# Delta net in a perceiver: the block inverse stops two quarters early, and a correction product takes the place of a transposition

## What is computed

```
q, k, v = silu(conv4(x @ W_qkv))            # q, k normalised to length 1
g = -exp(A_log) * softplus(a + dt_bias);  beta = sigmoid(b)
for t in range(S):                          # state: 128 x 128 per value head
    state = state * exp(g[t])
    delta = (v[t] - k[t] @ state) * beta[t]
    state = state + outer(k[t], delta)
    out[t] = q[t] @ state
y = rmsnorm(out) * norm_w * silu(x @ W_z);   x = x + y @ W_out
```

## Time and profile before

| | before |
|---|---|
| median of 3 runs | 1622.51 us (1621.43 to 1623.59) |
| profiled execution, time | 1629.97 us |
| profiled execution, span | 1628.0 us |
| PE busy | 1514.2 us, 93% |
| DVE busy | 1102.7 us, 68% |
| ACT busy | 607.5 us, 37% |
| POOL busy | 597.1 us, 37% |
| mean granted PE clock | 0.974 |

### The profile page before, as it was taken

How to read it: one execution, slowest core, us unless ns; L and a number is a source line. 1 busy time by engine, 2 the same in 40 slices (tenths; PEclk the granted TensorE clock), 3 DMA queues, 4 the chain that set the end, 5 groups by cost and what they waited for, 6 DMA issues and landing times. The chain is left out here.

```text
span 1628.0 us, 34641 instructions
## 1 busy us (share of the span) xinstructions
PE 1514.2 (93%) x14528; PEld 1075.3 (66%) x14528; DVE 1102.7 (68%) x1726; ACT 607.5 (37%) x1028; POOL 597.1 (37%) x935
## 2 busy tenths in 40 slices
PE   6799599999987889999999999999999978999999
PEld 3344278877964557777777677777777765555556
DVE  4767576687567677887788877788787834543433
ACT  3333353345343444344444445444444431111110
POOL 1201143254234457555564546645566421000000
PEclk9999899999998899999999999999999998999999
DMA  8533200110000222121211222112121114100000
GB/s 227 159 105 93 65 1 2 27 27 1 1 1 21 56 50 49 35 49 40 57 46 36 48 44 57 45 36 49 43 57 44 24 28 159 56 1 0 13 1 13
DMA packets 142347, 75.81 MB, mean 47 GB/s; under 512 B 111920, under 2 KB 123440, under 8 KB 140400
## 3 DMA queue, kind: packets, MB, share of 16 engines
q1 hardware_dynamic: 142192, 73.60, 17.6%
HBM read 55.73 MB, written 17.83 MB: 45 GB/s over the span
## 5 line engine op out<-in xcount | busy, mean ns | idle before, releaser
L1894 DVE SCALAR_TENSOR_TENSOR W<-PS,wc,W 128x504 f32<-128x504 f32 x375 | 274.8, 733 | 88.2 <-ACT W L1574 79.3
L1574 ACT ACTIVATE W<-PS,wc 128x512 f32<-128x512 f32 x125 | 85.8, 686 | 173.0 <-PE PS L1269 115.0
L2234 PE MATMUL PS<-HT,wgu 128*128 128x512 f32 x320 | 143.5, 593 | 0.0
L1269 PE MATMUL PS<-HT,wv 128*128 128x512 f32 x252 | 125.1, 620 | 3.4 <-DVE W L1894 3.4
L1441 PE MATMUL PS<-wo,ogT 128*128 128x256 f32 x512 | 119.1, 392 | 7.6 <-DVE dl L1958 5.1
L1292 PE MATMUL PS<-wz,HT 128*128 128x256 f32 x512 | 123.4, 389 | 0.6 <-DMA wz<-in_gdn_w 0.6
L1269 PE MATMUL PS<-HT,wkq 128*128 128x512 f32 x248 | 121.1, 613 | 0.8 <-DVE W L1894 0.8
L2368 DVE SCALAR_TENSOR_TENSOR act<-th,PS 128x512 f32<-128x512 f32 x48 | 33.0, 687 | 128.2 <-ACT th L2294 128.2
L1441 PEld LDWEIGHTS PS<-wo,ogT 128*128 128x128 f32 x512 | 98.6, 195 | 23.9 <-DVE dl L1958 5.3
L1794 POOL TENSOR_TENSOR rr<-nm,con 128x8 f32<-128x8 f32 x16 | 26.5, 1658 | 233.0 <-DVE nm L1923 233.0
L1578 ACT ACTIVATE W<-W 128x512 f32<-128x512 f32 x125 | 78.2, 626 | 89.7 <-DVE W L1894 89.7
(11 more groups left out here) (275 smaller groups left out, 3113.0 us busy)
## 6 DMA issues: line engine op xcount, KB each, us to landing
a_rows<-AT SPq DMA_DIRECT2D x16, 512.0 KB, 2.6
wk<-in_l0x_k SPq DMA_DIRECT2D x16, 384.0 KB, 3.8
wgu<-in_moe_gu SPq DMA_DIRECT2D x5, 1024.0 KB, 15.8
queries_scratch<-tts SPq DMA_DIRECT2D x32, 128.0 KB, 2.7
wkq<-in_gdn_w SPq DMA_DIRECT2D x16, 256.0 KB, 2.8
wv<-in_gdn_w SPq DMA_DIRECT2D x16, 256.0 KB, 2.8
wz<-in_gdn_w SPq DMA_DIRECT2D x16, 256.0 KB, 3.3
wo<-in_gdn_w SPq DMA_DIRECT2D x16, 256.0 KB, 2.9
```

Source lines behind the costliest of these rows:

```text
L1269: mm = pe.matmul(PS[:, qbank(h, q), :], w[:, o:o + DK], HT[:, k, f * 512:(f + 1) * 512], start=(k == 0), stop=(k == DC - 1))
L1574: a.activation(acc[:, flows(h, q), :], PS[:, qbank(h, q), :], ACT.Copy, scale=wc[:, h % 2, 4 * c + 3:4 * c + 4]).then_inc(s["tap"], 1)
L1894: v.scalar_tensor_tensor(a0, p0, wc[:, h % 2, 4 * c + 2 - k:4 * c + 3 - k], a0, ALU.mult, ALU.add).then_inc(s["conv"], 1)
L2234: mm = pe.matmul(PS[:, 2 * (i % 2) + w, :], pack[:, k, w, :], HT[:, k, f * N:(f + 1) * N], start=(k == 0), stop=(k == DC - 1))
```

## The change

The second transposition product and the second growing round go. Instead:

- all products of 64x64 matrices loop over n, b, hv, with the output of hv = 1 in the opposite half (`place`), so that four successive ones lie in four quarters; `cross` and `grow` write banks 6 and 7, one for each value head;
- the upper blocks of T alone are taken into `mix` (as if T were final but for the lower left 32x32 quarter), `lower_cross` makes the product that `cross(j, 5)` made, ACT keeps it (`keep_lower`, mask now with the sign -1) and keeps the rear 32 columns of the mixed product as `Zs` (`keep_Z`), and `correct` adds the product of the two (32 products with 64x32 weights, 32 columns moving) onto the mixed product in PSUM. `turn_T`, `keep_TT`, `TT`, `cross(j, 5)`, `grow(j, 5)` and the second `update` are gone;
- `blocks_in` sends the blocks in three parts: 4 transfers into T (q = 0, 2), the 8 into `TT16` (of which only q = 1, 3 are needed, each split by value head), then 4 into T (q = 1, 3, counted by `todd`). `load_out` moves behind `load_z` and `blocks_in`;
- the orders of PE, ACT, DVE and POOL queues are written anew, `gj` has two buffers, and PSUM banks 4, 5 and 6, 7 of the two `outs` results change places, with those of the two `turn_out`.

```diff
...
                 def blocks_in(h):
                     sp.wait_ge(s["sub"], h * NS + NS)
                     sp.dma_start(t_blocks[:, :, :, :], ti[:, :, :, :]).then_inc(s["d3"], 16)
                     sp.wait_ge(s["d3"], h * 16 + 16)
                     sp.wait_ge(s["zero"], h + 2)
-                    for q in range(S // SUB):
+                    for q in (0, 2):
                         for b in range(2):
+                            block_in(q, b, "t16")
+                    for q in (1, 3):
+                        for b in range(2):
                             k = (q * 2 + b) * 2 * TILES
-                            sp.dma_start(matrices(T[r:r + SUB, :, :, :])[:, :, q * SUB:(q + 1) * SUB],
-                                         t_blocks[k:k + 2 * TILES, 0, :, :].rearrange("m t s -> t m s")).then_inc(s["t16"], 16)
-                    for q in range(S // SUB):
+                            for hv in range(2):
+                                r = (b if hv == 0 else 1 - b) * S + q * SUB
+                                sp.dma_start(TT16[r:r + SUB, hv, :, q * SUB:(q + 1) * SUB],
+                                             t_blocks[k + hv * TILES:k + (hv + 1) * TILES, 1, :, :].rearrange("n t s -> t n s")).then_inc(s["u16"], 16)
+                    for q in (1, 3):
                         for b in range(2):
+                            block_in(q, b, "todd")
...
+                def place(hv, b):
+                    return 64 * b if hv == 0 else 64 * (1 - b)
+                def cross(j):
+                    pe.wait_ge(s["t16"], j * 64 + 64)
+                    if j + 1 < HK:
+                        pe.wait_ge(s["e"], j * 2 + 4)
+                    else:
+                        pe.wait_ge(s["xa"], j * 2 - 2)
                     for n in range(TILES):
                         for b in range(2):
+                            for hv in range(2):
+                                r, w = slice(64 * b, 64 * b + S), place(hv, b)
+                                mm = pe.matmul(PS[w:w + S, 6 + hv, n * 2 * SUB:(n + 1) * 2 * SUB], AT[r, j % 2, hv, n, :],
+                                               left(T[r, :, :, :])[:, hv * TILES + n, :, :], start=True, stop=True)
                     mm.then_inc(s["x"], 1)
+                def grow(j):
+                    pe.wait_ge(s["xs"], j * 3 + 2)
+                    pe.wait_ge(s["u16"], j * 128 + 128)
                     for n in range(TILES):
                         for b in range(2):
+                            for hv in range(2):
+                                r, w = slice(64 * b, 64 * b + S), place(hv, b)
+                                mm = pe.matmul(PS[r, 6 + hv, 256 + n * 2 * SUB:256 + (n + 1) * 2 * SUB], TT16[w:w + S, hv, n, :],
+                                               Xs[w:w + S, hv * TILES + n, :], start=True, stop=True)
+                    mm.then_inc(s["yy"], 1)
+                def lower_cross(j):
+                    pe.wait_ge(s["tu"], j + 1)
+                    pe.wait_ge(s["todd"], j * 64 + 64)
+                    for n in range(TILES):
+                        for b in range(2):
+                            for hv in range(2):
+                                r, w = slice(64 * b, 64 * b + S), place(hv, b)
+                                mm = pe.matmul(PS[w:w + S, 6 + hv, n * 2 * SUB:(n + 1) * 2 * SUB], AT[r, j % 2, hv, n, :], T[r, hv, n, 0:2 * SUB],
+                                               start=True, stop=True)
+                    mm.then_inc(s["x"], 1)
+                def mix(j):
+                    pe.wait_ge(s["pd"], j * 2 + 2)
+                    if j == 0:
+                        pe.wait_ge(s["z2"], 4)
+                    if j + 1 < HK:
+                        pe.wait_ge(s["dg"], j * 2 + 3)
+                    else:
+                        pe.wait_ge(s["ogs"], j * 2)
+                    for n in range(TILES):
+                        for b in range(2):
+                            for hv in range(2):
+                                r, w = slice(64 * b, 64 * b + S), place(hv, b)
+                                mm = pe.matmul(PS[w:w + S, 4 + hv, n * S:(n + 1) * S], T[r, hv, n, :], PT[r, j % 2, hv, n, :],
+                                               start=(n == 0), stop=(n == TILES - 1))
+                    mm.then_inc(s["mt"], 2)
+                def correct(j):
+                    pe.wait_ge(s["xs"], j * 3 + 3)
+                    pe.wait_ge(s["zs"], j + 1)
+                    for n in range(TILES):
+                        for b in range(2):
+                            for hv in range(2):
+                                w, m = place(hv, b), hv * TILES + n
+                                mm = pe.matmul(PS[w:w + 2 * SUB, 4 + hv, n * S + 2 * SUB:(n + 1) * S], Xs[w:w + S, m, :], Zs[w:w + S, hv, n, :],
+                                               start=False, stop=True, skip_group_check=True)
+                    mm.then_inc(s["ct"], 1)
...
                 def step(j):
                     h, g = j + 1, j - 1
+                    project(h, 0)
+                    project(h, 1)
                     turn_v(j, 1)
+                    decay_sums(h)
+                    project(h, 2)
+                    project(h, 3)
+                    turn_out(g, 0)
+                    cross(j)
+                    turn_out(g, 1)
+                    project(h, 4)
+                    grow(j)
+                    scores(h)
+                    project(h, 5)
+                    project(h, 6)
+                    lower_cross(j)
+                    mix(j)
                     project_z(j, 0)
+                    correct(j)
+                    project(h, 7)
+                    outs(j)
                     project_z(j, 1)
                     project_z(j, 2)
                     project_z(j, 3)
+                    for m in range(4):
+                        project_out(g, m)
+                    turn_v(h, 0)
...
+                def keep_X(j):
+                    a.wait_ge(s["x"], j * 2 + 1)
+                    for c in range(2):
+                        a.activation(Xs[:, :, c * SUB:(c + 1) * SUB].rearrange("p (h n) s -> p h n s", h=2),
+                                     PS[:, 6:8, 0:256].rearrange("p h (n c s) -> p h n c s", c=2, s=SUB)[:, :, :, c, :], ACT.Copy,
+                                     scale=C("rows")[:, c:c + 1]).then_inc(s["xs"], 1)
+                def keep_lower(j):
+                    a.wait_ge(s["x"], j * 2 + 2)
+                    a.activation(flat2(Xs[:, :, :]).rearrange("p (h n) -> p h n", h=2), PS[:, 6:8, 0:256], ACT.Copy, scale=C("rows")[:, 2:3]).then_inc(s["xs"], 1)
+                def keep_Z(j):
+                    a.wait_ge(s["mt"], j * 2 + 2)
+                    a.activation(matrices(Zs[:, :, :, :]), wide(4).rearrange("p (m s) -> p m s", s=S)[:, :, 2 * SUB:S],
+                                 ACT.Copy).then_inc(s["zs"], 1)
...
                 def step(j):
                     h, g = j + 1, j - 1
+                    tap(h, 0)
+                    tap(h, 1)
                     keep_v(j, 1)
+                    tanh(h, 0)
+                    tanh(h, 1)
+                    tap(h, 2)
+                    decays(h)
+                    tap(h, 3)
+                    keep_out(g, 0)
+                    tanh(h, 2)
+                    keep_X(j)
+                    tanh(h, 3)
+                    tap(h, 4)
+                    keep_out(g, 1)
+                    tanh(h, 4)
+                    tap(h, 5)
+                    tap(h, 6)
+                    keep_lower(j)
+                    keep_Z(j)
+                    tanh(h, 5)
                     tanh_z(j, 0)
+                    tap(h, 7)
+                    scale_wo(g)
                     tanh_z(j, 1)
+                    square_o(j, 0)
                     tanh_z(j, 2)
+                    square_o(j, 1)
+                    tanh(h, 6)
                     tanh_z(j, 3)
+                    swap_scale(h)
+                    tanh(h, 7)
+                    keep_v(h, 0)
...
+                def update(j):
+                    v.wait_ge(s["yy"], j + 1)
+                    t = T[:, :, :, :].rearrange("p h n (a c s) -> p h n a c s", a=2, c=2)[:, :, :, :, 0, :].rearrange("p h n a s -> p h (n a) s")
+                    v.tensor_tensor(t, t, PS[:, 6:8, 256:512].rearrange("p h (m s) -> p h m s", s=SUB), ALU.subtract).then_inc(s["tu"], 1)
                 def keep_M(j, hv):
-                    v.wait_ge(s["mt"], j * 2 + hv + 1)
+                    v.wait_ge(s["ct"], j + 1)
...
                 def step(j):
                     h, g = j + 1, j - 1
+                    conv(h, 0)
+                    conv(h, 1)
+                    silu(h, 0)
+                    silu(h, 1)
+                    conv(h, 2)
+                    conv(h, 3)
+                    silu(h, 2)
+                    silu(h, 3)
+                    conv(h, 4)
+                    update(j)
+                    norms(h)
+                    silu(h, 4)
```

(19 more changed lines are left out.)

312 lines of the change are left out of this document (61 added, 251 removed).

## The result

The change takes the kernel from 1623.05 us (median of 4 runs, 1621.43 to 1625.5) to **1547.78 us** (4 runs, 1547.26 to 1550.27): 75 us less, a ratio of 0.9538 with a 95% interval of 0.9522 to 0.9555. The forecast was 1524, 99 us less, with a range of 1505 to 1566.

A forecast was written before the change was run, and what follows sets the result against it. PE was taken as the bound: 43.9 us own work plus 0.7 and 0.5 of waits gives 45.1 a step, -87 us over 14 steps, -12 at the ends: 1622.5 - 99 = 1524 us; own range 1507 to 1539, stated 1505 to 1566.

The forecast's parts named there:

- What bounds the kernel, and what paces the small products: PE sets the step; weight loads pace the groups: 1.03 us each in four quarters, four groups -3.63, PE's own work 43.9.
- Rival C: The four quarters don't load weights at once, so the small-product groups stay at 1.9 us: 1580 us, chance 0.09.
- rival B: A limit for each PE record, 24 ns, so a small-product group takes 1.64 us: 1551 us, chance 0.09.
- The transfers: Blocks into T and `TT16` land before PE needs them; `cross` waits for 4, landed at 9.7 us against 10.4.
- Rival D: Slower than before: the odd blocks, last of 16 transfers, reach `lower_cross` late; 1650 us if 16 us late, chance 0.04.
- The margins of the second half: Waits before `correct`, `outs`, `project_out` and `turn_v` stay hidden, by 1.1, 0.4, 0.6 us, and 42.9 against 43.7.
- two `silu` fall into it ... +0.5: Two DVE `silu` run beside POOL's output scaling and slow down; `project(h, 4)` waits about 0.6 us: +0.5 us a step.
- +0.7 for `keep_out` behind `tap(h, 4)`: On ACT `keep_out(g, 1)` ends at about 16.0 us, so `scores`, due at 15.3, starts late: +0.7 us a step.
- One margin: POOL's `gates` finishes its halves at 8.3 and 10.2 us, ahead of the two `turn_out` at 9.5 and 11.5.
- the two ends: `first()` and `last()`, the delta net's partial steps, gain 6 us each, bounds 2 and 10: -12 us.
- the wait for `Xs`: PE's wait for ACT between `cross` and `grow` goes, covered by `turn_out` and `project(h, 4)`: -0.73 us a step.
- Rival A: DVE and ACT become the bound, a late `conv` moving all behind it; step 47.3 us: 1555 us, chance 0.19.

The follow-up runs named there:

- experiment 2: The changed kernel with hv outermost in `cross`, `grow`, `lower_cross` and `mix`, so that two quarters alternate: 1562.34 us, 0.9628 of before.
- Experiments 1: The kernel before with only `mix` looping over n, b, hv, so that it goes round four quarters: 1620.03 us, 0.9981 of before.
- experiment 7: The changed kernel with all 8 transfers into T ahead of the 8 into `TT16`, `cross` waiting for all 8: 1558.20 us, 0.9584 of before.
- experiment 4: The changed kernel with POOL scaling one tile of eight in each half of the gated output: 1525.72 us, 0.9397 of before.
- experiments 3 and 8: Changed kernel, `keep_out(g, 1)` before `tanh(h, 3)`: 1532.09 us; plus POOL's scaling's second half in four pieces: 1529.72; or both halves in two: 1528.96.

## Why the prediction was right, and where it was not

**What bounds the kernel, and what paces the small products: right.** Four groups were put at 1.03 us and took 0.95 to 1.13, `correct` at 1.03 and took 1.13. PE's own work in a step was put at 43.9 and measured 44.1. That the weights pace the groups has a comparison of its own in the new rows: with 32 columns moving and two places in use, 64 records take 1.78 us with 64 weight columns (`cross` in experiment 2) and 1.13 with 32 (`correct`); with 64 columns moving in place of 32 and the same weight columns, four quarters take 1.07 and 0.95 (`mix`, `lower_cross`). No run varied the weight columns alone. Rival C (quarters don't load at once) falls with these rows, and so does rival B: a group of 64 records in 0.95 us has 14.8 ns for each. By the Trainium skill's rule ("TensorE: Matmul & The Clock Gate", Part 1), starts at least 25 ns apart, 64 records would take 1.6; it does not hold for products in different quarters. The four together fell from 7.75 us to 4.21, by 3.5, where the sum has 3.63. Experiments 1 and 2 tie the larger part of it to the loop order: undoing the order alone costs 2.5 us a step. The other 1 us came with the groups' new places or banks, and which of them gives it was not tested.

**The transfers: right.** The last of the first four into T was put on its way at 7.1 us after `project(h, 0)`, measured 867.34 - 860.29 = 7.05 in SP's timeline of after:

```profile
865.54 1.80 SPq L1190 DMA_DIRECT2D T<-t_blocks  x4
867.38 3.76 SPq L1207 DMA_DIRECT2D TT<-t_blocks  x8
```

`cross` doesn't wait for them, nor `grow` or `lower_cross` for the others. Rival D did not occur. By experiment 7 the steps would have been as short without the split.

**The margins of the second half: right.** In all 13 steps there is no wait at `correct`, `outs`, `project_out` or `turn_v`, though only 0.4 to 1.1 us were to spare.

**The term that was too small: "two `silu` fall into it ... +0.5".** The mechanism and its place were right. The time was right for the step shown (the scaling was put at 6.4 to 10.2 us after `project(h, 0)` and ran from 6.4 to 10.6), while over the 13 steps it starts at 6.4 to 8.7. The size was not right. I took the 1.55 us that one `silu` had shown in before for each of the two. In the step shown the second took 2.38, because POOL's second half began as soon as the first `silu` was through, and it had to sit out nearly all of it; DVE lost 2.76 us there and 2.1 in the mean, not 1.7. The larger error is what this costs PE. I let part of it go "in place of the wait at `scores`", while it came on top of it: the late `conv(h, 3)` holds `tanh(h, 3)` on ACT, which the laid-out order leaves out, and `tap(h, 4)` and `keep_out(g, 1)` stand behind it, so the wait at `scores` grew from 0.72 (experiment 4) to 1.46. The scaling costs 1.6 us a step (experiment 4), against 0.5 in the sum: 1.1 x 14 = 15 us. The other term, +0.7 for `keep_out` behind `tap(h, 4)`, was right: 0.72 once the scaling is out of the way. In the mean of the steps the sum should have read 43.8 + 0.8 + 1.6 = 46.2.

**One margin was wrong in some steps.** The forecast had POOL's `gates` done 1.2 us or more ahead of each `turn_out` (8.3 against 9.5 us, 10.2 against 11.5). In three steps of 13 POOL starts its scaling 1.5 to 2.3 us later than in the step shown, behind the two `silu`, and `turn_out` waits for it.

**The rest of the gap.** In the cut of the traces the forecast would have 13 x 6.2 = 81 us in the steps and 18 at the two ends (one step and 12); measured were 66.2 and 13.6, of which 1.35 lie ahead of the delta net. So the ends lack 4.6 to 6 us. The new waits for `gates`, 4.96 for 1.10 in the first full step and 4.52 for 1.29 in `last()`, are the likely place; the forecast had named the first of them and not priced it, and that they are the whole of it was not tested. A small part of the steps' gap is the base as well: the wait for `Xs` that the sum takes off, 0.73, was that of one step, and its mean is 0.52. Together 19 of the 24 us. The other 4 to 5 are the base: the profiled execution of before lay 7.5 us above its median, that of after 2.5.

**Rival A was in part what happened.** Not that DVE or ACT had more work than PE, but a DVE queue in strict order that was put late in one place and had PE wait in three. Its price, 1555, was nearer to the result than the forecast's. The forecast's own range, 1507 to 1539, missed; the result lies in the stated one because that was made wide enough to take in A. Once this is eased (experiments 3 and 8), the kernel takes 1529 us, 96 us less than before on the same chip. What then comes last is POOL's chain.

## What to carry to other kernels

In this kernel the small products that share the array's quarters go at the pace that the loads of their weights explain, and the order of the innermost loop decides whether two or four quarters work at once; read it off a group's start to start, not its busy share. When a step is bound by one engine with the others a few us behind, a us taken from it is worth a us only until the next queue in strict order comes last: the same 2.4 us of PE work a step were worth 14 us in one kernel, and 27 (give or take 7) when two other queues had been eased. The steps of a hand-made pipeline can differ from one another within one execution, since two engines that race for something can come in either order. So read more than one step, and look at the granted clock of a step before explaining its length. A forecast of such a change should carry each held instruction's delay down to the last one that waits for it and add it to the waits that are there already.
